# DVE's state products of the second and third attention left in their PSUM bank and scanned from there, in a four-layer float32 transformer on one core

## What is computed

```python
    # L2A, per head: R = ((Q K^T) * decay^(i-j), i >= j) V ; a group norm of R ; R @ WO
    # L3A:
    dt = softplus(x @ Wdt + bdt)
    A_bar = exp(dt[..., None] * A)                          # 16 states
    x_db = x_ssm[..., None] * (dt[..., None] * Bm[..., None, :])
    h = scan(A_bar, x_db)                                   # h[t] = A_bar[t] * h[t-1] + x_db[t]
    y = einsum('bldn,bln->bld', h, C) * sigmoid(x @ Wz + bz)
    y @ Wout + bout
```

## Time and profile before

| | |
|---|---|
| median of 3 runs | 1229.63 us |
| the runs | 1228.03, 1229.63, 1231.99 us |
| the profiled execution, its own time | 1225.84 us |
| its span in the profile | 1223.8 us |
| mean granted TensorE clock | 0.926 of full speed |
| PE, DVE, ACT, POOL busy | 88%, 71%, 56%, 40% of the span |

### The profile page before, as it was taken

How to read it: one execution, slowest core, us unless ns; L and a number is a source line. 1 busy time by engine, 2 the same in 40 slices (tenths; PEclk the granted TensorE clock), 3 DMA queues, 4 the chain that set the end, 5 groups by cost and what they waited for, 6 DMA issues and landing times.

```text
span 1223.8 us, 18281 instructions
## 1 busy us (share of the span) xinstructions
PE 1082.9 (88%) x6855; PEld 654.4 (53%) x6855; DVE 872.7 (71%) x2050; ACT 685.5 (56%) x1155; POOL 493.8 (40%) x475
## 2 busy tenths in 40 slices
PE   7999999899999899999999867779899987659978
PEld 5766544344444354456444313464568676338868
DVE  4745547567666768788799899675686989966446
ACT  4477566686745586655676724562525786544221
POOL 2014122212213520184246456525455465686363
PEclk9999999999999789999999868769799998869989
DMA  8103000000000000000000000000514043147583
GB/s 257 57 9 138 1 1 0 1 1 2 1 1 18 1 2 1 20 1 1 18 1 1 0 0 1 1 3 33 172 52 166 33 164 112 33 168 232 209 291 92
DMA packets 36071, 70.14 MB, mean 57 GB/s; under 512 B 3088, under 2 KB 26128, under 8 KB 35472
## 3 DMA queue, kind: packets, MB, share of 16 engines
q0 software_dynamic: 9680, 45.88, 10.6%
q1 hardware_dynamic: 26304, 23.10, 6.0%
HBM read 59.34 MB, written 9.63 MB: 56 GB/s over the span
## 4 chain that ended last, share of the span: by engine, by line
PE 60%; DVE 14%; POOL 8%; ACT 8%; issue 6%; DMA 2%; another core or an unknown queue 1%; DVEq 0%; SPq 0%; POOLq 0%; ACTq 0%
PE ps L899 9%; PE ps L2177 5%; PE ps L1477 5%; PE ps L2185 3%; DVE own L2035 2%; PE ps L861 2%; PE ps L673 2%; PE ps L1276 2%; PE ps L1751 1%; PE ps L659 1%; POOL own L2059 1%; POOL own L1721 1%; PE ps L1455 1%; PE ps L1754 1%
## 5 line engine op out<-in xcount | busy, mean ns | idle before, releaser
L899 PE MATMUL ps<-own,g_f 128*128 128x512 f32 x320 | 147.8, 602 | 0.1
L899 PEld LDWEIGHTS ps<-own,g_f 128*128 128x128 f32 x320 | 59.2, 191 | 67.2 <-issue 61.0
L1226 POOL TENSOR_TENSOR own<-own 128x512 f32<-128x512 f32 x32 | 40.1, 1254 | 131.1 <-PE ps L899 95.5
L2035 DVE TENSOR_TENSOR_SCAN own<-own,carry 128x512 f32<-128x512 f32 x48 | 77.7, 1618 | 15.5 <-POOL own L2059 13.6
L2059 POOL TENSOR_TENSOR own<-own 128x512 f32<-128x512 f32 x32 | 50.7, 1585 | 53.2 <-ACT own L1985 53.0
L1939 PE MATMUL ps<-own,g_c 128*128 128x512 f32 x64 | 44.5, 784 | 30.5 <-POOL own L2065 30.4
L1976 ACT ACTIVATE own<-own,Acol 128x512 f32<-128x512 f32 x64 | 45.2, 714 | 40.1 <-PE ps L1939 38.9
L1895 POOL TENSOR_TENSOR own<-own 128x512 f32<-128x512 f32 x32 | 44.5, 1392 | 55.7 <-DVE own L1869 35.9
L1477 PE MATMUL ps<-g_l,own 128*128 128x512 f32 x128 | 59.5, 611 | 7.7 <-issue 7.3
L531 ACT ACTIVATE own<-xs,sm 128x128 f32<-128x128 f32 x128 | 52.5, 483 | 24.0 <-POOL sm L523 24.0
L2399 DVE TENSOR_TENSOR own<-ps,own 128x512 f32<-128x512 f32 x53 | 36.1, 682 | 41.4 <-PE ps L2177 13.3
(11 more groups left out here) (498 smaller groups left out, 2984.7 us busy)
## 6 DMA issues: line engine op xcount, KB each, us to landing
so<-own SPq DMA_DIRECT2D x10, 256.0 KB
g_l<-p_l SPq DMA_DIRECT2D x1, 2449.0 KB, 13.4
own<-sx SPq DMA_DIRECT2D x9, 256.0 KB, 9.5
g_f<-p_f SPq DMA_DIRECT2D x1, 2223.5 KB, 10.6
own<-cs SPq DMA_DIRECT2D x8, 256.0 KB, 3.4
sx<-brow SPq DMA_DIRECT2D x2, 960.0 KB, 12.4
g_l<-p_l SPq DMA_DIRECT2D x1, 1866.0 KB, 7.9
sx<-brow SPq DMA_DIRECT2D x1, 1472.0 KB, 14.3
```

Of the source, the lines that this page charges most:

```text
L899: x = e.matmul(s.bank["V%d%d%d" % (it, k, cc)][:, :], ew2[:, m, 128 * cc:128 * cc + 128], gm, start=False, stop=m == 3)
L2035: e.tensor_tensor_scan(H, A, H, init, ALU.mult, ALU.add).then_inc(*s.dve.up("H%d" % n))
```

## The change

For even n, DVE writes its product back into the bank it read (`fresh` is the bank), and the scan reads it there and writes the SBUF tile. For odd n nothing changes. With that, the wait for the SBUF tile stands before the scan and not before the product, and the bank is released by the scan (`scan%d`, `H%d`) and not by the product.

```diff
@@ l2a_tensor
-                    p = banks.take(s, q, "v%d" % n, (s.act if n % 2 else s.dve, "v%d" % n))
+                    p = banks.take(s, q, "v%d" % n, (s.act, "v%d" % n) if n % 2 else (s.dve, "scan%d" % n))
@@ l2a_vector
                     if n % 2:
                         yield
                         q.wait_ge(*s.pool("kv%d" % n))
+                        fresh = kv
                     else:
                         yield
                         q.wait_ge(*s.dve("qT"))
+                        q.wait_ge(*s.pe("v%d" % n))
+                        fresh = s.bank["v%d" % n][:, :]
+                        e.tensor_tensor(fresh, fresh, T[c][4], ALU.mult).then_inc(*s.dve.up("v%d" % n))
+                        yield
+                        q.wait_ge(*s.dve.now())
                         if n >= 4:
                             q.wait_ge(*s.pe("R%d" % (n - 4)))
-                        q.wait_ge(*s.pe("v%d" % n))
-                        e.tensor_tensor(kv, s.bank["v%d" % n][:, :], T[c][4], ALU.mult).then_inc(*s.dve.up("v%d" % n))
-                        yield
-                        q.wait_ge(*s.dve.now())
...
-                    e.tensor_tensor_scan(kv, decay.broadcast_to([128, W]), kv, init, ALU.mult, ALU.add).then_inc(*s.dve.up("scan%d" % n))
+                    e.tensor_tensor_scan(kv, decay.broadcast_to([128, W]), fresh, init, ALU.mult, ALU.add).then_inc(*s.dve.up("scan%d" % n))
@@ l3a_tensor
-                    p = banks.take(s, q, "B%d" % n, (s.act if n % 2 else s.dve, "B%d" % n))
+                    p = banks.take(s, q, "B%d" % n, (s.act, "B%d" % n) if n % 2 else (s.dve, "H%d" % n))
@@ l3a_vector
                     if n % 2:
                         yield
                         q.wait_ge(*s.pool("B%d" % n))
+                        fresh = H
                     else:
                         yield
                         q.wait_ge(*s.pe("B%d" % n))
+                        fresh = s.bank["B%d" % n][:, :]
+                        e.tensor_tensor(fresh, fresh, dx, ALU.mult).then_inc(*s.dve.up("B%d" % n))
+                        yield
+                        q.wait_ge(*s.dve.now())
                         if n >= 3:
                             q.wait_ge(*s.act("c%d" % (n - 3)))
                             q.wait_ge(*s.dve("C%d" % (n - 3)))
-                        e.tensor_tensor(H, s.bank["B%d" % n][:, :], dx, ALU.mult).then_inc(*s.dve.up("B%d" % n))
-                        yield
-                        q.wait_ge(*s.dve.now())
...
-                    e.tensor_tensor_scan(H, A, H, init, ALU.mult, ALU.add).then_inc(*s.dve.up("H%d" % n))
+                    e.tensor_tensor_scan(H, A, fresh, init, ALU.mult, ALU.add).then_inc(*s.dve.up("H%d" % n))
@@ ORDER, one of its four changed lines
-    "alffdakrgqkarapflfbbkgqhblkaplgbqbkagqflaafbkgqkbpialgkalqaaabffakkigqblpaakgqkfckfpkbaflhkaklpfclclamamhdldaddkfmmmmlhm"
+    "laffdakrgqkarapflfbbkgqhblkaplgbqbkagqflaafbkgqkbpialgkalqaaabffakkigqblpaakgqkfckfpkbaflhkaklpfclclamamhdldaddkfmmmmlhm"
```

More of the change, by code:

```diff
@@ L55 @@
     "aaanasnddnkfkkbffadllfppcfnlaaiakiaskqqaaakdiqfkakdffifppdkkdddfiqgkkanqbndgfknffkbsbllanbnbfppfnddgkglgnabdskggllggglaa"
-    "lalaailfkalifabkbffpplibblfgiqbgkgbkliaknbcfnfbfklbnggngqbknlqlnbcmlbbgkmgalbfpplcfbglglbgmqbaalqcgllbbglgglbgmbqlbcnqgm"
-    "blblglgglbgncqlbqkglfkpbbllbglbggblagqbkglaqkcblbgmgglglbqhlcqmgbmdrdilhlidrdikddildmbbcnhrcngkppcgngbmhclgqbpdmiqdhnlbp"
+    "lalaailfkalifabkbffppliblbfgiqbgkgbkliaknbcfnfbfklnggngbqkbnlqlnbmclbbgkmgalbfpplcfbglglbgmqbaalqcgllbbglgglbgmbqlbcnqgm"
+    "blblglgglbgncqlbqkglfkpbbllbglbgglbagqbkglaqkcblbgmgglglbqhlcqmgbmdrdilhlidrdikddildmbbcnhrcngkppcgngbmhclgqbpdmiqdhnlbp"
     "rfnrganplscsflcsmsialhhdmirmgidrdshndikkcqkirfdidmiciichnnimciirndmicibihnnidindrimidiiildiidknddbnnhinidrnhinnlidirkidd"
@@ L65 @@
     "shlslbbchmsbsmrbcgmribclvbqmcgshlbmqcmchclblhhmqhbbcblhmrdbmgrbbiqmgcmdllnchncdchhmdchdimridbmirhncminibnbbiiqnimbhnhhcm"
-    "chmcrlcgnrhlvmcbnmcqhmbcchnhcmdhbrhmlbrmdgcmbllbbqmhblhhmbdnbqgcmbhlbgnrcddbmrihisclhnbbmdnbirlcgnbnidlvbmbindcisbmdgdsd"
+    "chmcrlcgnrhlvmcbnmcqhmbcchnhmcdhbrhmlbrmdgcmbllbbqmhblhhmbdnbqgcmbhlbgnrcddbmrihisclhnbbmdnbirlcgnbnidlvbmbindcisbmdgdsd"
     "mdimdllbrnrnddrirlhlbnniilvicndsdhncsindqmmddqidmndqmmiiisnqhmmmcnsmmdqmmmqmdidmqndmqminrndnrnlriiinrissnldlrnlnrddlvrdd"
```

## The result

The changed kernel takes 1218.11 us (median of 10 runs, 1213.18 to 1225.15). The kernel before takes 1228.93 us in the runs beside it (median of 10, 1223.67 to 1231.99). The ratio is 0.991, with a 95% interval of 0.9887 to 0.9934: the change makes the kernel **11 us faster, 8 to 14**. The profiled execution took 1217.56 us, with a span of 1215.5 us, where the one before had 1225.8 and 1223.8.

A forecast was written before the change was run, and what follows sets the result against it. PE was taken as the bound overall, DVE at least as much in the third attentions. 1225.8 - 11.2 + 0.5 + 6.6 = 1221.7 us profiled, 4.1 us less, so 1225.5 us expected as the median; range 1218.4 to 1235.0 us.

The forecast's parts named there:

- The bound and the mechanism: PE bounds overall, DVE at least equally in the third attentions; SBUF-only DVE instructions and POOL stall each other, PSUM-input ones do not.
- The operands: Even products writing PSUM and scans reading it: 0.01 us more a scan, 0.5 us in all.
- The wait for the tile: On DVE, the SBUF tile wait moved from before the product to before the scan: costed at nothing.
- The bank waits: PE waiting for banks held until the scan ends: 27 late takings, 26.9 us, of which 6.6 us counts.
- the five: The five late bank takings on or right ahead of a piece of the chain, together 6.6 us.
- What counts is what lies on the chain. Four lengthened even scans lie there: 4.7 us: On DVE, of 14.3 us surplus on even scans only four on the chain that ended last count: 4.7 us saved.
- The sum of 11.2 us: Total saving forecast on the chain: 4.7 us from DVE's even scans plus 6.5 us from POOL's multiplies.
- POOL's share: 6.5 us: Eight POOL multiplies on the chain that began inside an even scan return to 1.26 us each: 6.5 us saved.
- The rival of cancelling: Half of the 11.2 us arrives and bank waits are paid in full: 1.5 us longer, 1231.1 us; chance 0.29.
- The rival of the bank waits: In PE's queue, 694 to 752 us: 60% of 26.9 us late takings is paid, 1235.0 us; chance 0.14.
- The slow in-place product: Each of 48 products reading and writing one bank takes 0.68 us more: 1240.5 us; chance 0.06.
- the POOL that is not freed: Scans still reading factor and start from SBUF still stall with POOL, so the 11.2 us stay: 1236.7 us; chance 0.03.

The follow-up runs named there:

- early_wait: The changed kernel with the wait for the SBUF tile put back ahead of the product; ratio 0.9885 to the kernel before.
- turns: The kernel before with only the change's order string, seven moved turns, banks still released by the product; ratio 0.9995 to the kernel before.
- replay_both: The changed kernel with delays put back on DVE's 25 scans and 25 POOL instructions that had taken longer before; ratio 0.9991 to the kernel before.
- replay_dve: The changed kernel with a reduction ahead of each of 25 scans, as long as its former stretch, 19.4 us in all; ratio 1.0017 to the kernel before.
- pad_pool2: The changed kernel with 352 tiny POOL memsets ahead of its 112 multiplies and sums, 14.0 us of measured delay; ratio 0.9876 to the kernel before.
- replay_pool: The changed kernel with 177 memsets ahead of the 25 POOL instructions that had taken longer before, 6.0 us of measured delay; ratio 0.9881 to the kernel before.
- pad_wide: The changed kernel with a 320-column DVE reduction of the bank between each even product and its scan; ratio 0.9974 to the kernel before.
- tight: The changed kernel with 31 turns moved so that each even scan stands right behind its product; ratio 0.9996 to the kernel before.
- pad_both: The changed kernel with 176 POOL memsets and a 320-column DVE reduction between each even product and its scan; ratio 1.0015 to the kernel before.
- banks: The kernel before with the change's order of turns and even banks released by the scan, product still to SBUF; ratios 1.0044 and 1.0069 to the kernel before.
- pad_pool: The changed kernel with 176 tiny POOL memsets ahead of its multiplies and sums, 8.6 us of measured delay; ratio 0.9891 to the kernel before.
- pad_behind: The changed kernel with a 320-column DVE reduction of a constant right behind each even scan; ratio 0.9927 to the kernel before.

## Why the prediction was wrong

**The bound and the mechanism** were read rightly. Even scans that read the bank are never held up (1.28 us at most in 48), nor do they hold up POOL. POOL's surplus at line 2059, now 2063, fell from 10.4 to 0.8 us. One detail of the reading does not fit its own rows: the scan at 731.76 is entered 0.03 us ahead of the multiply and is still the one that is held up, so a row's start does not always tell which of the two came second.

**The operands**: 0.01 us a scan, 0.5 us in all, were forecast. The scans take 1.275 us where the undisturbed odd ones and those of before take 1.28, and the product 0.689 instead of 0.678, 0.5 us over 48. The size of the term was right by chance, since another part of it is what costs. The Trainium skill, "VectorE: DVE Perf Modes", in the section on the TRN2 errata, gives instructions out of PSUM 62 cycles more of fixed time, by which, an estimate, the scans would have cost 3.1 us more. The trace does not agree: 1.275 us out of PSUM and 1.28 us out of SBUF.

**The wait for the tile** at nothing: no run contradicts it (early_wait). **The turns**, not priced: nothing (turns).

**The bank waits**, 6.6 us (6.5 by the rows, whose last term is 1.14 us and not 1.2): measured 5.4 and 8.5, with intervals of 1.7 to 9.2 and 5.2 to 11.7. They agree, and one of the five can be seen by itself: the second rotation was to wait 1.8 us for DVE's read of the first, and in the profile after PE stands for 1.88 us ahead of it. The method is worth keeping: every taking of a bank with its new releaser, but only what lies on a piece of the chain or right behind it.

**The step that failed is "What counts is what lies on the chain. Four lengthened even scans lie there: 4.7 us".** The sum of 11.2 us should have been 16 to 19. The scans' 4.7 us are worth 10 to 13 (replay_both, replay_dve). They are 19.4 us of delays in 25 places; most are not pieces of the chain that ended last, and yet they moved the end by 0.5 to 0.7 us for each microsecond. The chain is one path through the run as it was. Three strands share one DVE queue in strict order, and the likely way is that a scan that ends late delays the other strands behind it, the carry of its own number in the next chunk, and so pieces of the chain that bear another name; that it goes this way is argued and not shown.

**"POOL's share: 6.5 us"** is neither confirmed nor refuted. With 10 to 13 us for the scans, 3 to 9 are left of the 16 to 19, and 6.5 would fit in. Against it stands only that 14 us spread evenly (pad_pool2) and 6 us at the right places (replay_pool, no delay above 0.32 us) cost nothing.

The rival of cancelling argued that little of the 11.2 us would arrive, from the count that was too low already, and so it erred further in the same direction. The rival of the bank waits took 60% of 26.9 us; the runs showed a fifth to a third. The slow in-place product is excluded by the row of line 2028 above, the POOL that is not freed by the rows of line 2039 and of the multiply at 719.77.

As to what would show it: the mean of line 2035 was to fall from 1.60 towards 1.45 us; that of 2039 is 1.48, with the odd scans still stretched. POOL's multiplies and sums of over 2 us on the four lines went from 21 to 5.

## What to carry to other kernels

Count a stretch that two engines put on each other where it makes an instruction end late on which several strands hang, here a scan with its carry, and count it on and off the chain. The chain of one execution gives no upper bound for what such delays cost: 4.7 us of them lay on it, and all of them together were worth 10 to 13. Padding prices a delay only at the kind of place where it stands: 22 us behind the scans cost 2 us by the mark (6 beside pad_pool2), 23 us evenly ahead of the even ones about 10, 19.4 us ahead of 25 of them 10 to 13. And measure what the padding delays, from start to start in the trace, rather than adding up its rows: 17.8 us of memsets were 6.0 us of delay. As to the change itself, a scan that can read its input from PSUM while POOL works in SBUF was worth it here, with 5 to 9 us of bank waits to be paid.

## What the runs showed of the hardware

A product that reads and writes the same 128x512 fp32 bank in place takes 0.689 us, against 0.678 into SBUF. A scan with one tensor in PSUM and the other in SBUF takes 1.275 us (with a carry) and took 1.282 us at most in 48 instances, 36 of which overlapped a POOL multiply or sum. A reduction of a constant that is broadcast along the row takes 0.46 us for 320 columns, out of PSUM 0.484. A memset of two columns on POOL takes 0.1 us by its row, but nine in sequence delay what stands behind them by 0.3 us only (replay_pool).

The mean granted clock of TensorE differs between executions of one kernel, and the time with it: of the 12 runs of pad_wide the fastest had a clock of 0.928 and a span of 1218.2 us, the profiled one 0.912 and 1233.6 us. Busy by stretch, 700 to 1000 us (columns as in the earlier trace rows), of the kernel before, of the change and of replay_dve:

```profile
700.00:1000.00 300.00, 251.75 (x1703) 161.31 (x1702) 236.18 (x510) 146.68 (x270) 153.42 (x140) 0.86 0.18 60
```

```profile
700.00:1000.00 300.00, 258.31 (x1736) 168.99 (x1736) 227.04 (x514) 150.93 (x278) 146.86 (x142) 0.87 0.19 64
```

```profile
700.00:1000.00 300.00, 253.17 (x1668) 164.13 (x1666) 230.23 (x520) 143.70 (x266) 138.59 (x137) 0.84 0.17 56
```

Most kernels that lost the gain have lower means over their runs (replay_dve 0.921, replay_both 0.923, tight 0.924, pad_wide 0.920, pad_both 0.918, banks 0.921 and 0.922) than those that kept it (pad_pool 0.930, pad_pool2 0.931, replay_pool 0.930, early_wait 0.930). The change itself has 0.923 to 0.926, pad_behind 0.923, and the kernel before 0.925 to 0.930 beside them. Among the runs of one kernel, 0.01 of mean clock goes with about 8 us of time; this is an estimate, the common slope through the single runs of all the kernels here. By it, 7 of the 17 us between replay_dve and replay_pool go with the clock, and 4 to 5 of the 5.4 and 8.5 us of banks. So part of what later scans and bank waits cost may come by way of the clock. How much of it is cause and how much is only the longer time of a PE that waits is not told apart by any run here.
